# A gated recurrence of 2048 steps: both fp16 parts from one scan, z in two halves, r by a sigmoid

## The reference

```
z  = sigmoid(y_t W_z + h U_z + v_z)
r  = sigmoid(y_t W_r + h U_r + v_r)
hh = tanh(y_t W + (r h) U + v_h)
h  = (1 - z) h + z hh          (h is out_t - y_t)
```

## Time and profile before

| | |
|---|---|
| time, median of 3 runs (lowest, highest) | 6572.66 us (6569.87, 6573.13) |
| the profiled execution: its time, its span | 6569.49 us, 6567.7 us |
| TensorE busy (products, weight loads) | 5848.3 us (89%), 5500.4 us (84%) |
| VectorE busy, instructions | 5242.4 us (80%), 39096 |
| ScalarE busy, instructions | 3454.6 us (53%), 23405 |
| chain that ended last | VectorE 50%, TensorE 31%, ScalarE 10%, issue 8% |

### The profile page before, as it was taken

How to read it: one execution, slowest core, us unless ns; L and a number is a source line. 1 busy time by engine, 2 the same in 40 slices (tenths; PEclk the granted TensorE clock), 3 DMA queues, 4 the chain that set the end, 5 groups by cost and what they waited for, 6 DMA issues and landing times.

```text
span 6567.7 us, 486051 instructions
## 1 busy us (share of the span) xinstructions
PE 5848.3 (89%) x200312; PEld 5500.4 (84%) x200312; DVE 5242.4 (80%) x39096; ACT 3454.6 (53%) x23405; POOL 7.8 (0%) x22
## 2 busy tenths in 40 slices
PE   7888888888888888888888888888888888888888
PEld 7888888888888888888888888888888888888888
DVE  6888888878888888887888887888878888788887
ACT  3555555555555555555555555555555555555555
POOL 0000000000000000000000000000000000000000
PEclk8999999999999999999999999999999999999999
DMA  2000000000000000000000000000000000000000
GB/s 84 19 19 16 19 18 19 18 19 16 19 18 19 18 18 18 19 19 18 17 18 19 18 19 16 19 18 19 19 18 16 19 19 18 18 18 19 18 19 18
DMA packets 80316, 129.98 MB, mean 20 GB/s; under 512 B 12336, under 2 KB 18480, under 8 KB 80304
## 3 DMA queue, kind: packets, MB, share of 16 engines
q1 hardware_dynamic: 80304, 129.81, 5.7%
HBM read 20.46 MB, written 8.65 MB: 4 GB/s over the span
## 4 chain that ended last, share of the span: by engine, by line
DVE 50%; PE 31%; ACT 10%; issue 8%; DVEq 1%; POOL 0%; POOLq 0%
PE pair_r L299 31%; DVE rh_part L571 11%; DVE h_part L571 7%; DVE rh_part L578 7%; DVE pair_r L562 6%; DVE h_part L601 5%; DVE ps_z L562 5%; DVE pair_h L566 4%; ACT r_scan L434 4%; DVE h_part L609 3%; ACT pair_r L389 3%; ACT th_z L406 2%; DVEq L647 1%; PE ps_z L255 0%; DVE y_next L529 0%
## 5 line engine op out<-in xcount | busy, mean ns | idle before, releaser
L299 PEld LDWEIGHTS pair_r<-h_part,u_part 128*128 128x128 f16 x65568 | 1779.5, 96 | 1038.7 <-DVE h_part L571 1033.8
L299 PE MATMUL pair_r<-h_part,u_part 128*128 128x48 f16 (+1 forms) x65568 | 1976.9, 183 | 693.2 <-DVE h_part L571 686.5
L299 PE MATMUL pair_h<-rh_part,u_part 128*128 128x48 f16 (+1 forms) x65536 | 1953.4, 183 | 0.0
L299 PE MATMUL ps_z<-h_part,u_part 128*128 128x48 f16 (+1 forms) x65568 | 1942.9, 183 | 1.3 <-issue 1.3
L299 PEld LDWEIGHTS pair_h<-rh_part,u_part 128*128 128x128 f16 x65536 | 1797.6, 96 | 0.0
L299 PEld LDWEIGHTS ps_z<-h_part,u_part 128*128 128x128 f16 x65568 | 1784.7, 96 | 1.4 <-issue 1.4
L406 ACT ACTIVATE r_scan<-pair_r 128x4 f32<-128x4 f32 x4098 | 720.6, 176 | 1955.2 <-DVE pair_r L562 1752.6
L566 DVE TENSOR_REDUCE pair_h<-pair_h 128x4 f32<-128x8 f32 x4096 | 714.4, 175 | 549.9 <-PE pair_h L299 549.9
L562 DVE TENSOR_REDUCE pair_r<-pair_r 128x4 f32<-128x20 f32 x4098 | 766.5, 187 | 428.6 <-PE pair_r L299 2.7
L571 DVE TENSOR_TENSOR_SCAN rh_part<-r_scan,rh_part 128x12 f16<-128x12 f32 x4098 | 749.6, 183 | 140.5
L406 ACT ACTIVATE th_z<-ps_z 128x8 f32<-128x8 f32 x2048 | 362.7, 177 | 893.7 <-DVE ps_z L562 893.7
(11 more groups left out here) (75 smaller groups left out, 3111.3 us busy)
## 6 DMA issues: line engine op xcount, KB each, us to landing
w_stage<-w_in SPq DMA_DIRECT2D x384, 256.0 KB, 2.3
x_tok<-in_x SPq DMA_DIRECT2D x68, 128.0 KB, 2.6
out_dram<-o_tok SPq DMA_DIRECT2D x66, 128.0 KB, 2.3
mlp_w<-in_L_cond_W SPq DMA_DIRECT2D x2, 1024.0 KB, 6.8
u_raw<-in_L_cond_U_r SPq DMA_DIRECT2D x1, 1024.0 KB, 5.8
u_raw<-in_L_cond_U_z SPq DMA_DIRECT2D x1, 1024.0 KB, 7.8
u_raw<-in_L_cond_U SPq DMA_DIRECT2D x1, 1024.0 KB, 10.2
...
```

What stands on the lines that cost most here:

```text
L299: return nc.tensor.matmul(to[:, :, :, 0:run], u_part[:, g, part, k, gm * P:(gm + 1) * P], runs.unsqueeze(1).broadcast_to([P, repeats, n, r ...
```

## The change

- **One scan for both parts.** A value is now a run of STEP = 7 columns, and the scan goes over them with a factor and a term for each: state = factor x state + term, in fp32. The first column takes the share t (r, 1 - z, or hh); the second multiplies it by h (or by 2z, with hh) and adds a large constant, which rounds the sum to the bits that an fp16 part can hold; the third multiplies by a power of two and takes the constant off: that is the high part (HIGH = 2). The fourth and fifth turn it into t less high/h; this needs 1/h, or 1/(2z). The sixth multiplies by h again, which gives the low part, and the seventh scales it (LOW = 6). So one scan of 28 elements replaces a product of 4 and a scan of 12. The two reciprocals are new VectorE instructions (L598: 1/h for all 8 columns, of h_safe, which is h with bits set so that it isn't zero; L622: 1/(2z) for a half), with L617 (1 + tanh z, written twice) and L654 (h_safe). The constants lie in the operands' columns from the start.
- The moving operand has two runs of 24 (kept, new) instead of four of 12: 48 columns as before. The sums of r and z read 24 elements instead of 20 for 4 outputs, over two axes.
- **z in two halves.** pair_z has two banks; each half has its own products, its own sum, tanh and kept share. Bank ps_o is gone; its work moves to ps_p and pair_z.
- **r by a sigmoid**, written twice per value into r_term; the table set is loaded at the start. In the order of ScalarE's instructions there is one ACT_TABLE_LOAD, as before. z and the candidate keep tanh.
- `ahead` is 7 for R (was 5) and 2 for H (was 3). The seed of R always stands behind the first tanh of z.

The core of the diff:

```diff
-    ADDENDS = (2 * PARTS + 1, 2 * PARTS + 1, PARTS)
-    STEP, RUN, WIDE = 3, 12, 48
+    STREAMS = (PARTS, PARTS, 1)
+    STEP, HIGH, LOW, RUN, WIDE = 7, 2, 6, 24, 48
+    AGAIN = LOW - HIGH
     SLOT = WIDE + RUN
     PITCH = HS * STEP + RUN - B * STEP
-    KEEP, NEW = 0, PARTS
+    KEEP, NEW = 0, 1
...
-        r_scan = sb("r_scan", [P, S, STEP])
-        n_scan = sb("n_scan", [P, S, STEP])
-        h_cur, z_mul = r_scan[:, :, STEP - 1], n_scan[:, :, STEP - 1]
-        z_keep = r_scan[:, :, 1]
-        h_part = sb("h_part", [P, 2 * 2 * PARTS * PITCH + RUN], F16)
-        rh_part = sb("rh_part", [P, 2 * PARTS * PITCH + RUN], F16)
+        h_fac, z_fac = (sb(f"{n}_fac", [P, S, STEP]) for n in "hz")
+        r_term, k_term, n_term = (sb(f"{n}_term", [P, S, STEP]) for n in "rkn")
+        UP_H, UP_N = PART_SCALE / H_SCALE, PART_SCALE / 2
+        ROUND_H, ROUND_N = (1.5 * 2.0 ** 23 * bound / 2 ** 11 for bound in (H_SCALE, 2.0))
+        h_cur, z_two, z_keep, cand = h_fac[:, :, 1], z_fac[:, :, 1], k_term[:, :, 0], n_term[:, :, 0]
+        h_part = sb("h_part", [P, 2 * PARTS * PITCH + RUN], F16)
+        rh_part = sb("rh_part", [P, 2 * PITCH + RUN], F16)
...
+        def addends(banks):
...
+            runs = banks[:, 0:SLOT * HC].rearrange("p (m a c) -> p m a c", c=RUN, m=HC)[:, :, :, 0:B * STEP]
+            return runs.rearrange("p m a (b c) -> p m b a c", c=STEP)[:, :, :, :, HIGH:LOW + 1:AGAIN]
...
+            for t, up in ((h_fac, UP_H), (z_fac, UP_N)):
+                nc.gpsimd.memset(t[:, :, HIGH:LOW + 1:AGAIN], up)
+                nc.gpsimd.memset(t[:, :, HIGH + 1], -1.0 / up)
+            for t, rounding, up in ((r_term, ROUND_H, UP_H), (k_term, ROUND_H, UP_H), (n_term, ROUND_N, UP_N)):
+                nc.gpsimd.memset(t[:, :, 1], rounding)
+                nc.gpsimd.memset(t[:, :, HIGH], -rounding * up)
+            nc.gpsimd.memset(h_safe[:, :], 1.0).then_inc(s["safe_ok"], 1)
...
-                ahead = 5 if g == R else 3
+                ahead = 7 if g == R else 2
...
-            def update_gate():
-                tiles = [(m, k, part) for m in range(K) for k in range(K) for part in range(PARTS)]
+            def update_gate(hf):
+                tiles = [(m, k, part) for m in range(HC) for k in range(K) for part in range(PARTS)]
                 for n, (m, k, part) in enumerate(tiles):
-                    last = tile(ps_z, m, Z, m, k, part, h_part, n == 0, n == len(tiles) - 1)
-                last.then_inc(s["z_mm"], 1)
+                    last = tile(ps_z[hf], m, Z, hf * HC + m, k, part, h_part, n == 0, n == len(tiles) - 1)
+                last.then_inc(s[f"z{hf}_mm"], 1)
...
+            def reset_gate(hf, t1):
+                act.wait_ge(s[f"r{hf}_sum"], t1)
+                A(both(r_term[:, half[hf]]), twice(total_of(ps_r[hf], R)), ACT.Sigmoid, scale=scale_reg[R]).then_inc(s[f"r{hf}_in"], 1)
+            def update_gate(hf, t1):
+                act.wait_ge(s[f"z{hf}_sum"], t1)
+                A(th_z[:, half[hf]], total_of(ps_z[hf], Z), ACT.Tanh, scale=scale_reg[Z]).then_inc(s[f"z{hf}_th"], 1)
+            def kept_share(hf, t1):
+                act.wait_ge(s[f"z{hf}_th"], t1)
+                A(both(k_term[:, half[hf]]), twice(th_z[:, half[hf]]), ACT.Copy, scale=-0.5, bias=0.5).then_inc(s[f"keep{hf}"], 1)
+            def candidate(hf, t1):
+                act.wait_ge(s[f"h{hf}_sum"], t1)
+                A(both(n_term[:, half[hf]]), twice(total_of(ps_h[hf], H)), ACT.Tanh, scale=scale_reg[H]).then_inc(s[f"n{hf}_in"], 1)
...
-                        tanh(r_scan[:, half[hf], 1], ps_r[hf], R, HS, f"r{hf}_sum", t1, f"r{hf}_th")
+                        reset_gate(hf, t1)
                     A(hist[:, :, bass.ds(prv, 1)], h_cur.unsqueeze(2), ACT.Copy)
                     if proj is not None and u == K:
                         store_projection(proj[0], proj[1], 1).then_inc(s["xp_ok"], 1)
-                    tanh(th_z[:, :], ps_z, Z, S, "z_sum", t1, "z_th")
-                    storing = proj is not None and u % BODY == K
-                    if not storing:
-                        seed(pair_r, R, nxt)
-                    act.wait_ge(s["z_th"], t1)
-                    A(z_keep, th_z[:, :], ACT.Copy, scale=-0.5, bias=0.5).then_inc(s["z_keep"], 1)
-                    A(z_mul, th_z[:, :], ACT.Copy, scale=H_SCALE / 2, bias=H_SCALE / 2)
-                    if storing:
-                        seed(pair_r, R, nxt)
-                    tanh(n_scan[:, half[0], 1], ps_h[0], H, HS, "h0_sum", t1, "h0_th")
-                    seed(ps_z, Z, nxt)
-                    tanh(n_scan[:, half[1], 1], ps_h[1], H, HS, "h1_sum", t1, "h1_th")
+                    update_gate(0, t1)
+                    seed(pair_r, R, nxt)
+                    kept_share(0, t1)
+                    update_gate(1, t1)
+                    kept_share(1, t1)
+                    candidate(0, t1)
+                    seed(pair_z, Z, nxt)
+                    candidate(1, t1)
...
+            def total(banks, hf, name):
+                V.tensor_reduce(banks[hf][:, SUM:SUM + HS].rearrange("p (m b) -> p m b", b=B),
+                                addends(banks[hf]), AX_XY, ALU.add).then_inc(s[f"{name}{hf}_sum"], 1)
             def candidate_total(hf):
                 V.tensor_reduce(ps_h[hf][:, H_SUM:H_SUM + HS].rearrange("p (m b) -> p m b", b=B),
                                 candidate_cols(ps_h[hf]).rearrange("p m a b -> p m b a"), AX_X, ALU.add).then_inc(s[f"h{hf}_sum"], 1)
-            def low(parts, count, hi, hf, factors):
-                return V.tensor_tensor_scan(part_of(parts, count, hf, hi + 1), factors[:, half[hf]].rearrange("p s c -> p (s c)"),
-                                     part_of(parts, count, hf, hi), 0.0, ALU.mult, ALU.subtract)
+            def both_parts(to, hf, factors, terms):
+                return V.tensor_tensor_scan(to, factors[:, half[hf]].rearrange("p s c -> p (s c)"),
+                                            terms[:, half[hf]].rearrange("p s c -> p (s c)"), 0.0, ALU.mult, ALU.add)
             def gates(t1):
-                def gated_high(hf):
-                    dve.wait_ge(s[f"r{hf}_th"], t1)
-                    V.scalar_tensor_tensor(place(rh_part, PARTS, hf, 0), r_scan[:, half[hf], 1], 1.0,
-                                           h_cur[:, half[hf]], ALU.add, ALU.mult).then_inc(s[f"rhi{hf}"], 1)
-                def gated_low(hf):
-                    dve.wait_ge(s[f"rhi{hf}"], t1)
-                    low(rh_part, PARTS, 0, hf, r_scan).then_inc(s[f"rh{hf}"], 1)
-                for hf in range(2):
-                    dve.wait_ge(s[f"r{hf}_mm"], t1)
-                    total(ps_r[hf], R, HC, f"r{hf}_sum")
-                for hf in range(2):
-                    gated_high(hf)
-                    gated_low(hf)
-                dve.wait_ge(s["z_mm"], t1)
-                total(ps_z, Z, K, "z_sum")
+                dve.wait_ge(s["r0_mm"], t1)
+                total(ps_r, 0, "r")
+                dve.wait_ge(s["safe_ok"], t1)
+                V.reciprocal(h_fac[:, :, AGAIN], h_safe[:, :]).then_inc(s["r0_in"], 1)
+                dve.wait_ge(s["r1_mm"], t1)
+                total(ps_r, 1, "r")
+                def gated(hf):
+                    dve.wait_ge(s[f"r{hf}_in"], t1 if hf else (t1 * 2 if isinstance(t1, int) else dve.snap(t1 * 2)))
+                    both_parts(part_of(rh_part, 1, hf), hf, h_fac, r_term).then_inc(s[f"rh{hf}"], 1)
+                gated(0)
+                dve.wait_ge(s["z0_mm"], t1)
+                total(ps_z, 0, "z")
+                gated(1)
             def state(t1):
+                def z_twice(hf):
+                    dve.wait_ge(s[f"z{hf}_th"], t1)
+                    V.tensor_scalar(z_fac[:, half[hf], 1:AGAIN + 2:AGAIN], twice(th_z[:, half[hf]]), 1.0, TINY,
+                                    ALU.add, ALU.add).then_inc(s[f"z{hf}_two"], 1)
+                def z_inverse(hf):
+                    dve.wait_ge(s[f"z{hf}_two"], t1)
+                    V.reciprocal(z_fac[:, half[hf], AGAIN], z_two[:, half[hf]]).then_inc(s[f"n{hf}_in"], 1)
+                def kept(hf):
+                    dve.wait_ge(s[f"keep{hf}"], t1)
+                    both_parts(part_of(h_part, PARTS, hf, KEEP), hf, h_fac, k_term)
+                def new(hf):
+                    dve.wait_ge(s[f"n{hf}_in"], t2)
+                    both_parts(part_of(h_part, PARTS, hf, NEW), hf, z_fac, n_term).then_inc(s[f"hs{hf}"], 1)
+                t2 = dve.snap(t1 * 2)
+                dve.wait_ge(s["z1_mm"], t1)
+                total(ps_z, 1, "z")
+                z_twice(0)
                 dve.wait_ge(s["h0_mm"], t1)
                 candidate_total(0)
-                dve.wait_ge(s["z_keep"], t1)
-                V.tensor_tensor(keep_place(), by_half(z_keep), by_half(h_cur), ALU.mult).then_inc(s["khi"], 1)
-                def keep_low(hf):
-                    dve.wait_ge(s["khi"], t1)
-                    low(h_part, 2 * PARTS, KEEP, hf, r_scan)
-                def new_high(hf):
```

(25 more changed lines are left out.)

109 lines of the change are left out of this document (50 added, 59 removed).

## The result

The changed kernel takes **6168.69 us** (median of 4 runs, 6167.06 to 6169.82); the kernel before, on the same chip, 6572.51. The ratio is 0.9386, 95% interval 0.937 to 0.9402: 404 us less. The forecast was 6259, its range began at 6170.

What follows compares the result with a forecast made beforehand. A recurrence bounds the kernel: TensorE waits for the new state's scan. Five steps save 3 x 0.16 + 0.08 + 0.21 = 0.77 us, 296 over 384 fives, plus 18: 314 off 6569.5, adjusted by 3.2, gives 6259; range 6170 to 6440.

Steps and rivals of the forecast that it cites:

- rivals 1 to 4: Longer reciprocal 6300 (0.25); scan and reciprocal prices high 6485 (0.11); really long reciprocal 6882 (0.10); sigmoid table loads +5250 us (under 0.01).
- rival 5: Scan and reciprocal prices at their lower ends: plain step 2.94 us, back-edge step 3.09, total 6178 us; chance 0.03.
- turning steps: 32 x 4 steps outside the fives, one taken as a back-edge and three as plain: forecast 18 us saved.
- 2.72 + 0.21 + 0.05 = 2.98: Plain step: new scan's start, its length and the way to TensorE's weight load; 2.98 us against 3.14.
- It is the queue that holds it: Plain step's tail: VectorE's queue holds the new scan to 2.72, by 0.04 over the tanh, ready at 2.68.
- 2.50 for 1 + tanh(z), then 0.07 + 0.08 + 0.13 + 0.09 to the new scan: Step with VectorE's loop back-edge: new scan at 2.87, step 3.13 us, saving only 0.08.
- The storing step, 2.98: Step that stores the projection: seeds no longer ahead of candidate tanh, store delays only z's tanh; 2.98 us, saves 0.21.
- Between ends of 0.19 and 0.22 I take the middle: VectorE's scan of 28 elements, priced at 0.21 us, with 0.13 to the next start.
- The reciprocal, 0.16: VectorE's reciprocal of 4 elements, priced near a product: 0.16 us, 0.08 to the next start.
- 0.78: Start of r's first sum in a plain step, waiting for 23 products instead of 21: 0.78 us.
- Hidden, with 0.07 to spare: r's second scan reaches TensorE at 1.78, asked for after 10 products of H at 1.85.
- with 0.035 to spare: Second half's new state reaches TensorE 0.34 us after its restart, hidden by 15 products (0.375).

## Why the prediction was right and wrong

The direction and the place were right: one wait of TensorE's carries the gain, the high part's 0.19 was on the path of the tail, and rivals 1 to 4 did not come. What holds the new scan was wrong, and two terms of the sum were too large. The gain was too small by 90 us, and the time is 1.3 us under the range. It lies near the 6178 of rival 5, only in part for that rival's reason: the kept scan was as short as there, the new scan and the reciprocal were not, and what carried the time below 6178 is the back-edge, on which no rival stood. Step by step, the forecast had 15.05 for five steps (4 x 2.98 + 3.13); they take 14.83 (4 x 2.953 + 3.020). That is 0.22 x 384 = 84 of the 90. The turning steps gave 24 us where the forecast had 18.

- **"2.72 + 0.21 + 0.05 = 2.98" for a plain step: 2.95.** Four steps in five, 0.11 of the 0.22. The term that failed is the queue's: 0.13 from the kept scan to the second candidate sum. Measured 0.10 where the queue alone decides, in the step with the edge. In a plain step the queue is there at 2.60 and not at 2.63, so that the sum waits for its products, at 2.61; the scan follows at 2.69. "It is the queue that holds it" was wrong: without the reciprocals the sum stays at 2.61 and the time at 6166.
- **"2.50 for 1 + tanh(z), then 0.07 + 0.08 + 0.13 + 0.09 to the new scan", 3.13, for the back-edge: 3.02.** The other 0.11, from two places. First, I measured the edge from the *start* of the last VectorE instruction ahead of it (0.55). Before, that sum had waited for its products until it started. Now the scan ahead of the edge waits for the engine, not for a semaphore; from its start to the first instruction behind the edge it is 0.49. So 1 + tanh came at 2.43. Two other runs bear this reading out: with z as one nothing stands in front of this scan, and it starts as soon as its sigmoid is there, 0.06 earlier (1.45), yet the first instruction behind the edge stands at the same 2.01; with r by tanh the two are at 1.78 and 2.34 (means of the steps with the edge). So it is 0.55 again, counted from where the last wait ahead of the edge is over. Second, 0.33 to the new scan instead of 0.37: the second sum starts 0.10 behind the kept scan, and, waiting for nothing, takes 0.15 and lets the next start after 0.06.
- **The storing step, 2.98:** as a plain one, right; the order of seeds alone is 15 us in the kernel before.
- **The range.** Its lower end stood on rival 5, with 2.94 and 3.09. Plain steps did not reach that; the step with the edge is 0.07 under it, and this term alone is 27 us. The range had moved the prices of the scan and the reciprocal and left the 0.55 of the edge as it was.
- **"Between ends of 0.19 and 0.22 I take the middle":** the scans whose end is signalled take 0.212, as forecast; those of the new share took 183 ns before:

```profile
L571 DVE TENSOR_TENSOR_SCAN h_part<-n_scan,h_part 128x12 f16<-128x12 f32 x4096 | 748.8, 183 | 0.0
```

- The kept scans, which signal nobody, take 0.187 for 0.176 before: 11 ns for 16 elements, under my lower end of 17. The half-throughput rule of the Trainium skill ("DVE: opcode table, instruction layouts, handler registers and perf-mode slots", "6. Datapath and trigger behaviour") gives 33 ns for 16 elements, an estimate. The scans of the new share gained 29, near it, the kept ones 11. The missing signal does not explain the difference: without the reciprocals the kept scan signals nobody either and takes 201 ns on the mean, 0.21 in the tail shown above. What stands beside a scan in the queue moves its recorded duration by as much, and why stays open.
- **The reciprocal, 0.16:** 0.165. The iterative divide of the Trainium skill ("VectorE: DVE Perf Modes", "First, the fixed hardware budget") would have given 0.18 for four elements, an estimate. A reciprocal of 4 takes 0.175 for the first half and 0.156 for the second on the mean of the plain steps, and 0.149 where it is spare, a product of 4 0.155: the place moves it too, and for four elements no run sets it apart from a product. The reciprocal of 8 takes 206 ns, 41 more than that of 4, where a product of 8 took 151 and one of 4 155. The repeat count of 8 of the Trainium skill's section would make 33 ns of four more elements at 1.04 ns a pass, an estimate. So the growth is near the rule, and the duration for four elements does not show it.
- **r's first sum, "0.78":** 0.80. It does not wait for its products but stands behind h_safe in VectorE's queue (0.70, 0.17 long); with R's lead at 5 it stays at 0.80. It cost nothing, since r's path has room.
- **"Hidden, with 0.07 to spare" and "with 0.035 to spare":** right: TensorE does not stop there, and the experiments with tanh for the sigmoid and with R's lead, which use this room up, came as worked out from it: 6631 for 6630, 6225 for 6230.

What the forecast saw too simply is that the change is one design. Putting the tail's product back costs 413 us, tanh for the sigmoid 463, z as one 457: each more than the whole gain. The parts don't add; each brings its own path down to a point that the others reach too.
